# A scan step in three thirds: on every engine the three chains' instructions ahead of the scan's own

## The reference, cut to what matters

```python
x = x + _layernorm(_L0_attn_ref(_layernorm(x), ...))   # attention, 2 heads, relu on q, k, v and the output
x = x + _layernorm(_L0_ffn_ref(_layernorm(x), ...))    # 8 experts of 176, top 2, and a shared one
x = x + _layernorm(_L1_attn_ref(_layernorm(x), ...))   # state-space scan
x = x + _layernorm(_L1_ffn_ref(_layernorm(x), ...))    # ternary weights, squared relu, rms norm
```

```python
dA = jnp.exp(dlt.reshape(b, NC, DPG)[..., None] * A_g)
du = (dlt * u).reshape(b, NC, DPG)
state = dA * state + du[..., None] * Bs[:, :, None, :]
y = jnp.einsum('bgdn,bgn->bgd', state, Cs)
```

## Time and profile before

| | us |
|---|---|
| median of 3 runs | 2123.05 |
| lowest and highest | 2120.42, 2123.14 |
| the profiled execution, its time | 2119.12 |
| its span, first to last instruction | 2117.3 |
| busy in it: PE, DVE, ACT, POOL | 1652.8, 1770.3, 1035.2, 918.1 |
| mean granted clock of TensorE, full speed is 1 | 0.893 |

### The profile page before, as it was taken

One profiled execution on the slowest core, in us unless ns is written; L12 is line 12 of the kernel. 1 busy time (PEld: TensorE's weight loads), 2 busy tenths in 40 slices (PEclk: granted clock), 3 DMA queues, 4 the chain that ended last, 5 costly groups with the idle time before them and its releaser, 6 DMA issues. The chain is left out here.

```text
span 2117.3 us, 22566 instructions
## 1 busy us (share of the span) xinstructions
PE 1652.8 (78%) x5874; PEld 726.1 (34%) x5948; DVE 1770.3 (84%) x3142; ACT 1035.2 (49%) x1745; POOL 918.1 (43%) x676
## 2 busy tenths in 40 slices
PE   3463566868997789968997789977997799879856
PEld 1121122323352335413352325423452335234424
DVE  6566799989979998989989998899989987987830
ACT  3247233654547355644547355554647344834322
POOL 0103324464346534464346544465346544565520
PEclk9977686979998899979998899979998899889988
DMA  3001222312222222222222222222222223223300
GB/s 107 6 1 34 80 80 65 104 65 79 71 91 84 71 77 81 88 75 71 70 95 83 72 74 80 87 76 82 70 90 84 75 80 104 90 88 116 105 20 11
DMA packets 94601, 157.95 MB, mean 75 GB/s; under 512 B 10940, under 2 KB 23660, under 8 KB 94468
## 3 DMA queue, kind: packets, MB, share of 16 engines
q1 hardware_dynamic: 94468, 156.43, 22.8%
HBM read 143.83 MB, written 12.58 MB: 74 GB/s over the span
## 5 line engine op out<-in xcount | busy, mean ns | idle before, releaser
L1226 POOL TENSOR_TENSOR prod<-state,c_all 128x512 f32<-128x512 f32 x512 | 675.1, 1323 | 731.4 <-DVE state L1203 665.4
L1203 DVE TENSOR_TENSOR_SCAN state<-decay,ps_b 128x512 f32<-128x512 f32 x512 | 619.3, 1209 | 9.3 <-issue 0.4
L750 PE MATMUL ps_y<-prod,idf 128*128 128x512 f32 x1024 | 617.0, 696 | 4.6 <-DVE u L1216 3.6
L1210 DVE TENSOR_TENSOR ps_b<-du,ps_b 128x512 f32<-128x512 f32 x512 | 347.4, 678 | 89.1 <-PE ps_b L743 88.8
L919 ACT ACTIVATE decay<-delta,a_neg 128x512 f32<-128x512 f32 x512 | 359.5, 719 | 36.0 <-DVE state L1203 33.0
L743 PE MATMUL ps_b<-b_rows,sel_b 48*128 48x512 bf16 x512 | 211.6, 414 | 173.8 <-DVE state L1203 169.2
L750 PEld LDWEIGHTS ps_y<-prod,idf 128*128 128x128 f32 x1024 | 186.2, 210 | 136.7 <-issue 110.4
L743 PEld LDWEIGHTS ps_b<-b_rows,sel_b 48*128 48x128 bf16 x512 | 47.8, 94 | 492.6 <-DVE state L1203 355.0
L619 PE MATMUL ps_x<-xT,w 128*128 128x512 bf16 (+1 forms) x393 | 129.8, 415 | 81.3 <-DVE arena_l L1095 71.3
L826 ACT ACTIVATE arena_l<-ps_x 128x512 f32<-128x512 f32 (+1 forms) x104 | 61.8, 594 | 194.2 <-PE ps_x L619 193.7
L535 PE MATMUL ps_x<-hT,win 128*128 128x512 bf16 (+1 forms) x456 | 136.0, 442 | 23.6 <-DVE arena_b L1171 18.7
(11 more groups left out here) (230 smaller groups left out, 2415.7 us busy)
## 6 DMA issues: line engine op xcount, KB each, us to landing
c_all<-c_rows SPq DMA_DIRECT2D x512, 256.0 KB
c_rows<-arena_l SPq DMA_DIRECT2D x32, 256.0 KB
out<-arena_b SPq DMA_DIRECT2D x8, 512.0 KB
x_in<-in_base SPq DMA_DIRECT2D x8, 256.0 KB
c_all<-in_winT SPq DMA_DIRECT2D x1, 1280.0 KB, 7.3
arena_b<-in_w_fc SPq DMA_DIRECT2D x1, 1024.0 KB, 12.4
arena_b<-in_w_proj SPq DMA_DIRECT2D x1, 1024.0 KB, 8.3
w<-in_w1T SPq DMA_DIRECT2D x1, 792.0 KB, 5.8
```

The source lines that it names most:

```text
L750: nc.tensor.matmul(ps_y[:], idf[:], prod[:, n % NP, :], start=(n % NST == 0), stop=(n % NST == NST - 1)).then_inc(reduced, 1)
L1203: nc.vector.tensor_tensor_scan(state[:, n % NS, :], decay[:, n % NDA, :], ps_b[:, n % NDB, :], 0.0, ALU.mult, ALU.add).then_inc(scanned, 1)
L1210: nc.vector.tensor_tensor(ps_b[:, j % NDB, :], du[:, slot(s, ct), :], ps_b[:, j % NDB, :], ALU.mult).then_inc(driven, 1)
L1226: nc.gpsimd.tensor_tensor(prod[:, n % NP, :], state[:, n % NS, :], c_all[:, n % NC, :], ALU.mult).then_inc(multiplied, 1)
```

## The change

In each third, the scan's instruction goes behind those of the chains, on every engine:

```diff
             for k, (j, part, _) in enumerate(SLOTS):
-                fns["scan"](eng, s, j, part)
                 for slots in chains:
                     run_steps(e, eng, fns, slots[k])
+                fns["scan"](eng, s, j, part)
```

## The result

| | before | changed |
|---|---|---|
| median of the runs, us | 2123.1 (2120.42 to 2123.32, 4 runs) | 2098.43 (2095.19 to 2099.69, 4 runs) |
| ratio, 95% interval | | 0.9884 [0.9867, 0.9901] |
| profiled execution: time / span, us | 2119.12 / 2117.3 | 2098.59 / 2096.8 |
| mean granted clock | 0.893 | 0.904 |

A forecast was written before the change was run, and what follows sets the result against it. DVE was taken as the bound, except in a PE-bound stretch. Terms 9.8 - 8.8 + 5.1 - 5.0 + 0.6 + 3.0 = +4.7 us on 2123.05 gave about 2128 us, range 2108 to 2144.

The forecast's parts named there:

- the +3.0 for places that I did not walk: Unexamined places where chain matmuls now precede a b with under a microsecond in hand: 0.5 us in six iterations.
- DVE instructions that run while POOL does: Overlap of DVE and POOL instructions, whose lengths change with their places; left out of the +4.7 us sum.
- rival (a): DVE stalls beside POOL's product shrink: 30 us less, 11 more for L994, giving 2109 us; chance 0.23.
- the first L984 of the pair: Two L984 right behind a scan: one done before the product started, the second ending with it; 1.60 us for both.
- Begin of iteration 0, -5.0: w_fc's load goes ahead of five loads of C on SP, so DVE's 8.29 us wait shrinks by 5.
- Head, +9.8: Start of iterations 1 to 7: step 1's b goes behind wout's first half, its drive 1.4 us later each.
- End, -8.8: End of eight iterations: silu L1171 moves ahead of step 62's scan, the last y comes about 1.1 us earlier.
- Middle, +5.1: End of the PE-bound stretch: chain work moves ahead of b, step 47's scan 0.85 us later in six iterations.
- w_proj, +0.6: Iteration 0: w_proj's load keeps its queue place while the chain comes to it earlier; 0 to +1.2 us.
- ACT and POOL, 0: Decays are two steps ahead and products wait for the scan anyway, so the moved chain steps cost 0.
- no effect of principle: Whole loop: chain work between scan instructions stays the same on average, so only particular places change.

The follow-up runs named there:

- the load alone: Kernel before, with only the w_fc load issued ahead of the scan's c_all loads on SP in step 0 of iteration 0: 2114.48 us, 0.9959.

## Why the prediction was wrong

Its forecast was the sum of waits, +4.7 us. For waits inside the loop that came close: +9.8 - 8.8 + 5.1 + 0.6 + 3.0 = +9.7, and DVE's idle time there rose by 10.0. That they meet so nearly is in part luck: the head's waits came to 15.4 us and not 9.8, the +3.0 for places that I did not walk is not to be seen (the waits for a b rose by 22.1, of which head and middle are 21.9), and the waits for the down projection and at L1081 fell by 6.6, which no term had. What failed is one step that was left out and one that was too small.

**"DVE instructions that run while POOL does": left out of the sum.** This is the step that gave the wrong sign. DVE's busy time fell by 22.9 us. It was named, as rival (a), with chance 0.23 and 19 us net (30 less, 11 more), and put at nothing in the sum; it should have been part of the forecast. The argument against it, that a second instruction behind a scan runs into the product, holds for some kinds and was no reason to hold the sum at zero. Its parts: L994 +11 forecast, +11.3 measured; the 56 of L1128, L1124 and L1121 -16.8, measured -11.6 for the three groups; L1175 -13.6, measured only -3.9, since I put its stalls down to the product where most were beside L1248 or L1252, which belong to a chain. Together the parts on the list came to -4.2 us and not -19. Not on the list were L984 and L973, -7.4 each, two pieces of the gate, L1032 and L1041, +12, and -18 net in many other kinds, small ones of the gate and the norms above all (L1000 -4.6, L1010 -3.6, two casts at L942 -6.0); by groups it is -25.5, since records overlap a little. So rival (a) had the mechanism and the sign, and its size by luck.

In this case's traces either side is held up by the other: the cast of 0.16 us takes 1.18 behind a product, and the product takes 1.73 us behind L1175. The rule that I weighed there (the Trainium skill, SBUF — State Buffer, "Who interferes with whom": an exclusive lock, whoever is first has it for the whole instruction) agrees with both. I had written that POOL was not shown blocked; the changed trace shows it, and L1252 with 1.82 us in the trace of before did so already. Nor was the first L984 of the pair in the earlier trace rows done before the product started: it started at 1064.57, the product at 1064.73, and such an instruction takes 0.35 us. It had only started first.

**Begin of iteration 0, -5.0.** The mechanism was right and the size was off: -9.4 in the trace, -8.7 by the load alone. I bounded the landing by w_proj's 8.3 us; it took 6.1 with no load of C ahead of it, so that the whole wait went, and one microsecond beside it.

**Head, +9.8.** Right in kind; undoing it gave 6.6 us, within the measurement of the forecast. The forecast of 1.4 a head was too low for the wait itself, 1.18 to 3.27 and 2.2 on average, in part since I took wout's half at its 3.72 us everywhere and it took 5.41 to 5.81 in three of the seven; in time less than half of the waits came back.

**End, -8.8.** The waits for the last y did fall, from 25.5 to 16.1 us, but undoing the move of the scan gave back only 4.0 of them, and cost nothing in time. The walk moved L1171 and L1041 and has no word of L1032, which moves ahead of the scan with L1171. In the changed trace L1032 came behind a product's start, and L1041, at 1162.56, behind that of L1252 (1.13 us instead of 0.16).

**Middle, +5.1.** Undone, 6.5 us of waits go and no time that can be told.

**w_proj, +0.6.** Its wait went from 4.1 to 4.9.

**ACT and POOL, 0.** Wrong by 12 us of DVE's busy time (1747.4 with their new lists, 1735.3 with the old), with the time 4 us apart, which is within the measurement. I looked at whether they were late, and not at when POOL would be in DVE's way. With PE's old list decays were late too, by 7.6 us in all.

Iterations 2 to 5 came out within half a microsecond each of before, as the forecast of "no effect of principle" would have it. Iteration 0 did not, since there nothing took the stalls' place: its idle time fell by 1.4 us while DVE was busy 6.3 us less. Why its waits did not rise as elsewhere is not shown.

## What to carry to other kernels

When an order of instructions changes, price the overlaps of each engine pair that hinders itself before the waits: compare, for each kind of DVE instruction, its shortest with its mean time, and see which ones the new order puts just behind the start of a GpSimd instruction. Look up which GpSimd instruction that is: one that moves along with them hinders them as before. A small one counts as much as a large one there, since it takes as long as the other has left. And an order need not be the same on all engines: the engine that bounds can take the one that keeps it clear of the other, while its suppliers keep theirs. A wait removed by moving a supplier's instruction is only gained if what it moved past is not wanted too: three b put back in an iteration gained 6.6 us (uncertain by 5), PE's whole list put back nothing.

## What the runs showed of the hardware

In these traces it is not the size of a DVE instruction that decides whether one of POOL hinders it. No instruction with an operand in PSUM was hindered among those looked at. In the kernel before, over all records, shortest, median and longest:

```profile
L1210 DVE TENSOR_TENSOR ps_b<-du,ps_b x512: 661/675/697, 210.2 to 2021.7; 128x512 f32<-128x512 f32 x171
L1171 DVE SCALAR_TENSOR_TENSOR arena_b<-arena_b,ps_x x32: 655/674/690, 400.2 to 2024.3; 128x512 f32<-128x512 f32 x32
L1175 DVE TENSOR_TENSOR u<-u,arena_b x32: 673/694/1801, 405.7 to 2027.9; 128x512 f32<-128x512 f32 x32
```

The 512 drives, which read one operand from PSUM, never take more than 0.70 us, though many run beside a product (in the changed kernel the one at 1161.21, 0.68 us, beside the product of 1160.68); L1175, with both operands in SBUF, takes up to 1.80. The scans read their b from PSUM: in the changed kernel 104 of the 512 stood for at least half their length beside a POOL instruction, and all 512 took 1.18 to 1.22 us. To have everything in SBUF is not enough to be hindered either: the statistics of the norms that read x_in, arena_e or x (L497, one input of 128x256 bf16) took 0.40 to 0.43 us in every record of either kernel. The same page and section of the Trainium skill (SBUF — State Buffer, "Who interferes with whom") says that two SBUF inputs contend, that at most one does not, and that a cast or tensor_scalar can in its fast mode. These rows agree.

A load of 1 MB, that of w_fc, landed in 5.8 to 7.3 us in the kernels that issue no load of C just before it, and in 11.8 to 13.0 in the four that issue five of them, of 256 KB each, just before it.
